# Two experts' Gelus in every second turn, and the hidden normalisation on ScalarE, in a fused Mamba and mixture-of-experts kernel

## The reference

```python
xn = layernorm(x)
# Mamba: projection, causal convolution of 4 taps, silu, then per feature 16 states
h = h * exp(dt * A) + (dt * xt) * Bt          # a scan over 1024 tokens of each of 8 sequences
y = (sum over states of h * Ct) + xt * D
mamba = layernorm((y * silu(gate)) @ W_out + b_out + xn)
# experts: top 2 of 8
h = gelu(layernorm(xn @ w1[e] + b1[e]) * g1[e] + be1[e])   # 512 hidden features
expert = sum over the two experts of weight * (h @ w2[e] + b2[e])
out = x + mamba + layernorm(expert + xn)
```

## Time and profile before

| | us |
|---|---|
| median of 3 runs | 1838.35 (1836.94 to 1839.93) |
| the profiled execution | 1839.68 |
| its span, first to last instruction | 1837.7 |
| busy: PE, VectorE, ScalarE, GpSimd | 1580.6, 1545.9, 1458.0, 968.3 |
| the loop of 128 turns (234 to 1608 us of the span) | 1374 |
| the seven tiles behind it (1608 to 1690) | 82 |

### The profile page before, as it was taken

The page is one execution under the profiler, slowest core; times in us unless marked ns, Lnnn a source line. Parts: engine busy times, 40 slices in busy tenths (PEclk is TensorE's granted clock), DMA queues, the critical chain, the costliest instruction groups (busy, mean ns, idle before and its releaser), DMA issues.

```text
span 1837.7 us, 28368 instructions
## 1 busy us (share of the span) xinstructions
PE 1580.6 (86%) x6978; PEld 967.1 (53%) x6978; DVE 1545.9 (84%) x2529; ACT 1458.0 (79%) x2552; POOL 968.3 (53%) x563
## 2 busy tenths in 40 slices
PE   5988389898889888998989898889898998975899
PEld 4555145555556555555555555555555655542344
DVE  4767489999999998989998989999998989811997
ACT  3545379898988989898988889898989898944676
POOL 2767756565555556556655565565556555612000
PEclk9777789999999999999999999999999999988899
DMA  7999743433433333334343333333333333323984
GB/s 236 346 290 350 256 112 83 106 97 83 110 82 93 96 93 85 105 85 107 83 108 91 87 97 91 98 83 100 89 94 85 105 85 108 82 39 75 276 270 148
DMA packets 182857, 234.69 MB, mean 128 GB/s; under 512 B 45865, under 2 KB 148524, under 8 KB 182719
## 3 DMA queue, kind: packets, MB, share of 16 engines
q1 hardware_dynamic: 141234, 171.83, 30.3%
q0 software_dynamic: 26160, 36.06, 10.5%
q10 hardware_dynamic: 15328, 25.20, 4.1%
HBM read 149.33 MB, written 83.70 MB: 127 GB/s over the span
## 4 chain that ended last, share of the span: by engine, by line
DVE 33%; ACT 25%; PE 21%; issue 13%; DMA 4%; ACTq 3%; POOL 1%; SPq 0%; another core or an unknown queue 0%; DVEq 0%; POOLq 0%
DVE area L1276 7%; DVE area L1289 5%; ACT area L660 4%; DVE area L1306 4%; DVE area L1285 3%; PE psX L975 3%; ACT psD L654 3%; PE psT L1023 3%; DVE more L1338 3%; ACT h_T L694 3%; ACT L702 3%; ACT L699 3%; DMA area<-L_attn_x 2%; DVE more L1335 2%; DVE h_norm L1319 2%
## 5 line engine op out<-in xcount | busy, mean ns | idle before, releaser
L539 POOL TENSOR_TENSOR area<-area,more 128x1024 f32<-128x1024 f32 x258 | 604.4, 2360 | 553.2 <-DVE area L1289 279.2
L1306 DVE TENSOR_TENSOR area<-area,psD 128x1024 f32<-128x1024 f32 x256 | 310.1, 1211 | 0.2 <-PE psD L988 0.2
L965 PE MATMUL psH<-w_sb,ffn_xT 128*128 x544 | 265.8, 612 | 5.8 <-ACT ffn_xT L670 5.7
L975 PE MATMUL psX<-w_sb,h_T 128*128 x1088 | 267.0, 389 | 0.8 <-ACT y_out L676 0.8
L516 POOL DMA_INDIRECT expert_d<-y_out,meta x139 | 220.7, 1588 | 83.3 <-ACT y_out L676 56.9
L996 PE MATMUL psY<-ident,area 128*128 128x128 f32 x2048 | 250.7, 276 | 0.0
L975 PEld LDWEIGHTS psX<-w_sb,h_T 128*128 128x128 f32 x1088 | 205.8, 193 | 60.6 <-issue 32.4
L660 ACT ACTIVATE area<-area,A_sb 128x512 f32<-128x512 f32 x258 | 171.5, 712 | 74.2 <-DVE area L1289 40.8
L996 PEld LDWEIGHTS psY<-ident,area 128*128 128x128 f32 x2048 | 222.2, 141 | 13.4
L694 ACT ACTIVATE h_T<-psT,be_T,g_T 128x128 f32<-128x128 f32 x540 | 202.2, 459 | 4.7 <-PE psT L955 4.7
L654 ACT ACTIVATE psD<-area,A_sb 128x512 f32<-128x512 f32 x258 | 177.9, 690 | 31.6 <-DVE area L1276 12.3
(11 more groups left out here) (186 smaller groups left out, 2515.4 us busy)
## 6 DMA issues: line engine op xcount, KB each, us to landing
more<-B_rows_d SPq DMA_DIRECT2D x130, 512.0 KB, 4.0
xin<-sorted_x SPq DMA_DIRECT2D x137, 128.0 KB, 2.1
more<-ssm_d SPq DMA_DIRECT2D x18, 512.0 KB, 3.7
area<-xnT_d SPq DMA_DIRECT2D x17, 512.0 KB, 3.5
mamba_d<-mo_stage SPq DMA_DIRECT2D x17, 512.0 KB, 2.9
area<-L_attn_x SPq DMA_DIRECT2D x8, 1024.0 KB, 6.9
xnT_d<-w_sb ACTq DMA_DIRECT2D x16, 512.0 KB, 6.6
expert_d<-area ACTq DMA_DIRECT2D x8, 1024.0 KB, 8.9
```

The costliest lines, as they stand in the source:

```text
L539: pool.tensor_tensor(inflow[:, k], dtx, B_rep[par][:, k].rearrange("p (a t) -> p a t", a=1).to_broadcast([P, KD, CHUNK]), ALU.mult).then_i ...
L965: nc.tensor.matmul(psH[:, :], ffn_xT[:, k, :], w1_sb[:, bass.ds(e, 1), k, :].rearrange("p o h -> p (o h)"), start=(k == 0), stop=False)
L975: nc.tensor.matmul(psX[:, DIM:2 * DIM], h_T[:, buf, k, :], w2_sb[:, bass.ds(e, 1), k, :].rearrange("p o d -> p (o d)"), start=(k == 0), st ...
L1306: V.tensor_tensor(h, h, C_rep[k].rearrange("p (a t) -> p a t", a=1) .to_broadcast([P, KD, CHUNK]), ALU.mult).then_inc(S[f"hC{k}_done"], 1)
```

## The change

The hidden normalisation leaves VectorE. VectorE computes minus the mean (`neg_mean`), and ScalarE, after the root, makes the shift `-mean * root` (`hnm`, one column) and then scales and shifts the 512 columns of `psH` in one instruction. The normalised tile has two buffers, the Gelu's output three, and `LAG` is 3 where it was 2.

ScalarE runs no Gelu in odd turns. In even turns it loads the Gelu table, runs the Gelus of tile u-1 and of tile u, and loads the exp table again. The gate's Silu stands in turn 1 with the one of the convolution, with one exp table load behind both. `copy_y` moves ahead of the Gelus.

On PE the order of a turn is new. In even turns: `up(u+1)`, C0, `transpose_h(u)`, `transpose_x`, (in turn 0 the transposed sum), C1, `down(u-2)`, `add_up`, and the task last. In odd turns: `up(u+1)`, C0, `transpose_x`, C1, the task, `down(u-2)`, `add_up`, and last, once ScalarE has taken the task out of `psT`, `transpose_h(u)`.

Behind the loop, SP issues the tile loads before it waits for the last mamba output; GpSimd's first scatter of zeros and PE's first dummy transposes are gone; PE does `up(u+1)` before `transpose_h(u)`.

```diff
-LAG = 2
+LAG = 3
-            store_mamba(CHUNKS)
             for u in range(MAMBA_TURNS, FFN_TURNS):
                 load_tile(u + 2, (u + 2) % RING)
+            store_mamba(CHUNKS)
...
+            def hidden_norm(u):
+                act.wait_ge(S["rstd_ready"], u + 1)
+                act.wait_ge(S["mean_ready"], u + 1)
+                nc.scalar.activation(hnm[:, :], neg_mean[:, :], ACT.Copy, scale=hrs[:, 0:1]).then_inc(S["shift_ready"], 1)
+                act.wait_ge(S["shift_ready"], u + 1)
+                if u >= 2:
+                    act.wait_ge(S["hT_done"], u - 1)
+                nc.scalar.activation(h_norms[u % 2], psH[:, :], ACT.Identity, scale=hrs[:, 0:1], bias=hnm[:, 0:1]
+                                     ).then_inc(S["norm_done"], 1)
...
                         hidden_root(u)
+                        hidden_norm(u)
...
                         copy_xT(u + 1)
+                        if u >= LAG:
+                            copy_y(u - LAG)
...
-                        with_gelu()
-                        copy_y(u, (pr - LAG) % RING, pr % 2, e_y)
-                        gelu(u, pr % 2, e)
+                        if pr % 2 == 0:
+                            with_gelu()
+                            if u > 0:
+                                gelu(u - 1)
+                            gelu(u)
+                            with_exp()
                         if pr == CONV_TURN:
+                            gate_silu_of(c, half)
                             act.wait_ge(S["seed_done"], g + 1)
                             conv_silu(g)
-                        if pr == GATE_TURN:
-                            gate_silu_of(c, half)
-                        with_exp()
+                            with_exp()
...
+                        up(u + 1)
                         spread_C0(u + 1, state[0], par, g)
+                        if pr % 2 == 0:
+                            if u > 0:
+                                transpose_h(u)
                             transpose_x(u + 2)
+                            if pr == 0:
+                                transpose_sum(c)
+                            early_C = pr not in (CONV_TURN - 1, DT_TAKEN + 1)
+                            if early_C:
+                                spread_C1(u + 1, state[1], par)
+                            if u >= 2:
+                                down(u - 2)
+                            if not early_C:
+                                spread_C1(u + 1, state[1], par)
+                            if pr == 0:
+                                seed(c)
+                            add_up(u, pr % 2)
+                            if TASKS[pr] is not None:
+                                pe.wait_ge(S["gelu_done"], u + 1)
+                                task(TASKS[pr], g)
                         else:
+                            early_C = pr != CONV_TURN
+                            if early_C:
+                                transpose_x(u + 2)
+                                spread_C1(u + 1, state[1], par)
+                            pe.wait_ge(S["gelu_done"], u)
...
+                            if u >= 2:
+                                down(u - 2)
+                            add_up(u, pr % 2)
+                            wait_taken(TASKS[pr], g)
+                            transpose_h(u)
...
                 V.bn_aggr(hmv[:, :], hstats[:, :]).then_inc(S["var_ready"], 1)
-            def hidden_norm(u):
-                dve.wait_ge(S["rstd_ready"], u + 1)
-                dve.wait_ge(S["hT_done"], u + 1)
-                V.tensor_scalar(h_norm[:, :], psH[:, :], hmv[:, 0:1], hrs[:, 0:1], ALU.subtract, ALU.mult
-                                ).then_inc(S["norm_done"], 1)
+                dve.wait_ge(S["var_ready"], u + 1)
+                V.tensor_scalar(neg_mean[:, :], hmv[:, 0:1], -1.0, None, ALU.mult).then_inc(S["mean_ready"], 1)
```

More of the change, by code:

```diff
@@ L55 @@
 CONV_TURN = 1
-GATE_TURN = 2
 DT_TAKEN = TASKS.index("dt1") + 1
@@ L784, in _ @@
                         par = half if pr < PAIRS - 1 else ahead
-                        e, e_y = expert(u), expert(u - LAG)
                         decay0_of(u + 1, 0, state[0], g, par)
@@ L817, in _ @@
             for u in range(MAMBA_TURNS, FFN_TURNS):
[L818 removed]
                 copy_xT(u + 1)
                 hidden_root(u)
+                hidden_norm(u)
+                copy_y(u - LAG)
                 with_gelu()
[L822 to L823 removed]
+                if u == MAMBA_TURNS:
+                    gelu(u - 1)
+                gelu(u)
                 with_exp()
@@ L827, in _ @@
                         take_out(CHUNKS, j, psY[:, j * CHUNK:(j + 1) * CHUNK])
-            for u in range(FFN_TURNS, FFN_TURNS + LAG):
-                copy_y(u, (u - LAG) % RING, u % 2, expert(u - LAG))
+            for t in range(FFN_TURNS - LAG, FFN_TURNS):
+                copy_y(t)
             def root(k, off):
@@ L874, in _ @@
         def _(pe):
-            for name, ahead in (("tr_ready", 1), ("sum_done", 2), ("hT_done", 1)):
+            for name, ahead in (("tr_ready", 1), ("sum_done", 2)):
                 pe.sem_inc(S[name], ahead)
@@ L941, in transpose_x @@
                 pe.wait_ge(S["xin_loaded"], 32 * (t + 1))
-                if not (isinstance(t, int) and t == 0):
+                if t > 0:
                     pe.wait_ge(S["xT_copied"], t)
-                if not (isinstance(t, int) and t < 2):
-                    pe.wait_ge(S["y_copied"], t - 1 + 1)
+                if t >= LAG + 2:
+                    pe.wait_ge(S["y_copied"], t - 1 - LAG)
                 for k in range(KD):
@@ L1069, in _ @@
             transpose_x(0)
-            for k in range(KD):
-                m = nc.tensor.transpose(psX[:, DIM + k * P:DIM + (k + 1) * P], ident[:, :], ident[:, :])
-            m.then_inc(S["y_ready"], 1)
             pe.wait_ge(S["w_ffn"], W_FFN)
             pe.wait_ge(S["b_rows_in"], 48)
-            up(0, expert(0))
+            up(0)
             transpose_x(1)
@@ L1103, in _ @@
-                        if pr == TASKS.index("out0"):
-                            project_out(c, 0, psT[:, :])
-                        elif pr == TASKS.index("out1"):
-                            project_out(c, 1, psT[:, :])
-                        elif TASKS[pr] is not None:
-                            task(TASKS[pr], g)
-                        if not early_C:
-                            transpose_x(u + 2)
-                            spread_C1(u + 1, state[1], par)
-                        down(u - 1, (pr + 1) % 2, e_down)
@@ L1125, in _ @@
                 transpose_x(u + 2)
-                down(u - 1, (u - 1) % 2, e_down)
-            down(FFN_TURNS - 1, (FFN_TURNS - 1) % 2, expert(FFN_TURNS - 1))
+                down(u - 2)
+            for t in range(FFN_TURNS - 2, FFN_TURNS):
+                down(t)
             pe.wait_ge(S["mo_copied"], 2 * CHUNKS + 2)
@@ L1441, in _ @@
             gate(CHUNKS, 1)
-            with dve.Fori(MAMBA_TURNS, FFN_TURNS) as u:
+            for u in range(MAMBA_TURNS, FFN_TURNS):
                 hidden_stats(u)
-                hidden_norm(u)
             dve.wait_ge(S["w_end"], 16 * len(end_loads))
```

130 lines of the change are left out of this document (69 added, 61 removed).

## The result

The changed kernel takes 1958.02 us (median of 4 runs, 1952.34 to 1959.27) against 1839.14 for the kernel before: 1.0636 times as long, 95% interval 1.0606 to 1.0667. The execution profiled is the shortest of the four, 1952.34 us with a span of 1950.6.

A forecast was written before the change was run, and what follows sets the result against it. VectorE leads before, TensorE and ScalarE within 5%; after, a serial two-turn chain through ScalarE, with PE late. Pairs sum to 92.2 against 85.9 a chunk, 101 us for 16, plus 6 behind the loop: 1945 us; range 1850 to 1985.

The forecast's parts named there:

- Table loads: ScalarE's function table loads in the loop: 18 a chunk become 10, saving 10.4 us a chunk, with no drain.
- Norm on ScalarE: Shift, scaling and longer root steps added on ScalarE: 1.10 us a turn, 8.8 a chunk.
- The gap: ScalarE between paired Gelus: waits for PE's transposes and two hand-overs, 0.84 us, four times a chunk, 3.4.
- (0,1): Turns 0 and 1 of a chunk: VectorE leads at 24.2 us, gate 2.6 late by PE's transposed sum, 26.8.
- (2,3): Turns 2 and 3: serial chain 18.2 us plus takes, residue of B and C +1.15, bc task 0.4 late; 21.5.
- (4,5): Turns 4 and 5: chain 18.2 us, takes 1.15 and 1.15, two half copies 1.2, dt1 0.5 late; 22.2.
- (6,7): Turns 6 and 7: PE's 13.2 us with the out projection ends last, then Gelu and decays follow; 21.7.
- Behind the loop: Expert tiles after the loop: longer turns +5.5, Gelu 127 +2.35, late scatters +2.9, early loads -4.3; sum +6 us.
- PE never late: Rival for the loop: PE's matmuls close up and it delays nothing; about 1852 us, chance 0.12.
- VectorE leads: Rival for the loop: ScalarE's chain stays under VectorE's pair, each turn saves 1.17 us; 1695 or 1775, chance 0.13.
- The clock: Rival for PE: more waiting lowers its clock once every chunk; about 1999 us, or 1972 with half, chance 0.10.
- Switches cost more: Rival for ScalarE: each of 128 removed table switches also took a drain as long as its load; 1780 us, chance 0.01.

The follow-up runs named there:

- sum-first run: Changed kernel with PE's transposes of the sum put ahead of the transposes of h in turn 0 of a chunk; 1932.4 us.
- the run with the transposes before the sum: Changed kernel with PE's transposes of h put ahead of the adding up in odd turns; 1.0705 times the kernel before.
- the scaling alone: Kernel before with only the shift and scaling of the hidden tile moved to ScalarE, Gelus still in every turn; 1923.6 us.

## Why the prediction was right, point by point

The time, 1958 against 1945, and the main mechanism were right: ScalarE gives the saved table loads back, in the shift, the scaling and the gap between the Gelus, and all of it stands in blocks for which the scans wait. That the number is so near is in part luck: at full clock the pairs are shorter than forecast, and falls of the clock, which the sum left out, fill the difference.

*Table loads.* With those for the Silus there are 176 from the loop on (88, 71, 16 and 1 by line) against 304 (136, 135, 17 and 16): 128 fewer, as predicted, of 1.283 us each as before. No drain is seen, behind a load or ahead of one: the first Gelu starts at 1029.23, with a load from 1027.94 of 1.28 before it, and the second load starts at 1033.19, with the Gelus from 1031.66 of 1.50 before it. The rule of a drain of 1.38 us (the Trainium skill, "ScalarE: Activation LUTs", "What ACT_TABLE_LOAD costs") isn't borne out by either trace.

*Norm on ScalarE.* Predicted 0.31 + 0.68 + 0.11 a turn; measured 0.33 and 0.68 to the next instruction, the root 0.54. The scaling lasts 0.78 us, near the 0.81 it took on VectorE. By the experiments it costs 2.3 us a chunk in the changed kernel and 4.8 in the kernel before, so the parts don't add: 4.8 and 4.3 alone, 6.6 together.

*The gap.* Predicted 0.84, measured 0.92 to 1.15, mean 0.98: mostly the hand-overs, 0.16 and 0.05 in my estimate, were short by 0.14 together. The block was put at 7.0 with the `copy_y` of 0.49; it is 7.0 (6.54 and `copy_y` 0.47), and 7.2 where the gap is 1.15.

*VectorE's negation.* 0.154 us long, with a step of some 0.1 to 0.2; 0.20 was right.

*The pairs.* (0,1) 26.8 predicted, 26.8 to 27.1 measured, and the sum-first run shows its cause, though the gate waits 1.6 us on average, not 2.6; some of the lateness is handed on. (2,3) 21.5, measured 21.0 to 21.4; the term of 1.15 for the residue shows there (moved away, the pair loses 1.2), but 0.8 comes back in (4,5). (4,5) 22.2, measured 21.9. (6,7) 21.7, measured 20.5 or 21.0 at full clock and 22.1 to 22.7 with a fall. The four sum to 92.2 against 92.37, because errors cancel: without the falls it would be about 90.8. The wait for a decay, forecast at 2 to 3 us before the first scans of even turns, is 1.2 us in turn 0 and 1.9 in turn 6; ahead of turn 4 it stands before the residue, 4.3.

Which engine ends last in (6,7) can be read from the two kinds of chunk. ScalarE in turn 6 without and with the fall:

```profile
494.95 0.38 ACT L674 ACTIVATE ffn_xT<-psX 128x256 f32<-128x256 f32 x1 [0.66 <-PE psX L1007]
500.12 1.50 ACT L713 ACTIVATE h_T<-psT,be_T,g_T 128x128 f32<-128x128 f32 x4 [1.15 <-PE psT L981]
...
675.92 0.60 ACT L746 ACTIVATE mo_stage<-psT 128x512 f32<-128x512 f32 x1 [1.06 <-PE psT L1084]
678.14 0.38 ACT L674 ACTIVATE ffn_xT<-psX 128x256 f32<-128x256 f32 x1 [1.04 <-PE psX L1007]
683.30 1.50 ACT L713 ACTIVATE area<-psT,be_T,g_T 128x128 f32<-128x128 f32 x4 [1.15 <-PE psT L981]
```

PE, made 1.6 us late by the fall, makes the pair 1.6 longer, so PE does end last there, as predicted, but at another place: ScalarE waits for it before the take of the output and the copy of x, which stands behind `down`. The gap before the second Gelu, where the prediction let PE's chain end behind its sum and the transposes, is 1.15 either way. That also fits the run with the transposes before the sum, which left the pair as it was at full clock.

*Behind the loop.* This term was mis-sized: +6 predicted, +16.4 measured. Rows of the changed kernel:

```profile
1757.29 1.55 POOL L526 DMA_INDIRECT expert_d<-y_out,meta  x1 [8.03 <-ACT y_out L681]
...
1763.60 0.78 ACT L703 ACTIVATE h_norm<-psH,hnm,hrs 128x512 f32<-128x512 f32 x1
...
1764.62 2.83 PE L993 MATMUL psH<-w_sb,ffn_xT 128*128 x4 [3.00 <-ACT h_norm L703]
...
1765.05 1.55 POOL L526 DMA_INDIRECT expert_d<-y_out,meta  x1 [6.21 <-ACT y_out L681]
```

The turn from 1757.29 to 1765.05 is 7.76, as predicted (7.7). The next is 9.58: PE, waiting 3 us in it, works part of it at its lower clock (granted 0.82, and 0.87 over the stretch), and the first layer takes 2.83 instead of 1.98 us. By the scatters, the five turns in the middle take 44.6 us instead of 34.0. Two of them, without a fall, are 7.76 and 8.05, near the forecast; three with one are 9.6. So about half of these 10.6 us is the longer order that was forecast, and the other half is the clock, which the sum had at nothing. Up to the first of these turns the changed kernel is 2.1 us ahead, with the loads (-4.7, shown) and the Gelu of tile 127 in it. Behind the last it is 7.9 behind: the third scatter, 4.5, and a first one that comes 7.8 us after the last turn's scatter, not 4.7; the prediction had 2.9 for all of it. By the runs, the scaling on ScalarE is 5.6 of the whole (103.6 against 98.0) and the order 2.1, where stretches with the same code differ by up to 1.6 from run to run.

*The rivals.* PE never late (1852): out, PE's waits and the run with the transposes before the sum show it on the path. VectorE leads (1695 to 1775): out by the scaling alone. The clock (1972 to 1999): partly true. In the loop it is granted 0.97 against 0.99, one or two falls of 3.4 us in each chunk. Where one meets the pair (6,7) it costs 1.6 us, by estimate 1.1 us a chunk more than in the kernel before, some 18 us in the loop, and some 5 behind it. It did not decide the result, since 5.5 us a chunk remain at full clock, but by the same estimate the time without it would have been nearer 1935. Switches cost more (1780): out.

## What to carry to other kernels

Joining two uses of a function table pays only where the instructions joined are ready together. Here the second Gelu shared one PSUM bank with the first, so ScalarE stood for the transposes each time, and the join cost more than the loads it saved. The two Silus, which were ready, gained. Before moving work from a leading engine to one that is busy 5% less, ask what waits behind it there: VectorE's scaling was 0.81 us in an engine that waited anyway, on ScalarE it delayed the decays of every scan. And of several edits made together, time each alone: one of these was a gain, hidden under two losses. Before a mean over chunks is explained, look at the single ones: here they fall into two groups, with and without a fall of TensorE's clock.

## What the runs showed of the hardware

GpSimd's products and some of VectorE's instructions shut each other out. In the changed kernel GpSimd runs two products from 1043.35 for 4.68 us, to 1048.03:

```profile
1043.35 4.68 POOL L544 TENSOR_TENSOR area<-area,more 128x1024 f32<-128x1024 f32 x2 [4.56 <-DVE area L1328]
```

and VectorE beside it:

```profile
1044.40 2.35 DVE L1349 TENSOR_TENSOR area<-area,psD 128x1024 f32<-128x1024 f32 x2
1046.67 2.44 DVE L1399 TENSOR_TENSOR area<-area,more 128x1024 f32<-128x1024 f32 x1
```

The products with C, of which one operand is in PSUM, keep their 1.2 us each. L1399, both operands in SBUF, takes 2.44 us where the same instruction took 1.22 in the kernel before. 1.36 us of waiting for the products and 1.22 of work would be 2.58, near the 2.44. GpSimd's product stays at 2.36. The Trainium skill, "SBUF — State Buffer", section "Who interferes with whom", gives these two engines one shared port pair with an exclusive lock, and the rows agree. The residue, moved by one turn, likewise went from 0.69 to 1.59 us, and the first tap of the convolution from 1.32 on average to 1.79. This is one more price of changing an order: which pairs of instructions meet.

A fall of the granted clock in a chain of short waits costs nearly its whole loss: in the 3.4 us at 1.2 GHz from 669.93 PE falls 1.6 us behind, and the pair of turns is 1.6 us longer. The same fall elsewhere costs nothing: at 43.6 to 46 us after turn 0 it left (4,5) at 21.9.

The head of the program, with its many transfers, took 77.5 us longer in the profiled execution on one of the three chips (the medians of the kernel before differ by 68.7) while its loop took the same time to 0.01 us a chunk. Why isn't shown. Ratios from different chips stand for different times.
